# Folding V into Wo for two batches at once, with the contraction filled by stacked Wo parts, from batch 4 on

## What is computed

```
x = x + xattn(x)            q from x, k and v from the normalised 64 context rows
    qk   = einsum('bihd,bjhd->bhij', q, k) * attn_scale
    attn = softmax(qk)
    out  = einsum('bhij,bjhd->bihd', attn, v).reshape(b, -1, 1024) @ Wout
x = x + tanh(layernorm(x) @ W @ aux1 @ aux2 + bias)
```

## Time and profile before

| | |
|---|---|
| median of 3 runs | 2052.41 us (2051.54 to 2052.84) |
| the profiled execution, span | 2049.4 us |
| PE busy | 2024.3 us, 9168 matmuls |
| DVE, ACT, POOL busy | 1523.8, 1320.3, 1342.0 us |
| share of the 16 DMA engines | 74.3% |
| granted TensorE clock | 0.999, at 2.4 GHz |

### The profile page before, as it was taken

The page is one execution under the profiler, slowest core; times in us unless marked ns, Lnnn a source line. Parts: engine busy times, 40 slices in busy tenths (PEclk is TensorE's granted clock), DMA queues, the critical chain, the costliest instruction groups (busy, mean ns, idle before and its releaser), DMA issues.

```text
span 2049.4 us, 31334 instructions
## 1 busy us (share of the span) xinstructions
PE 2024.3 (99%) x9168; PEld 1679.8 (82%) x9168; DVE 1523.8 (74%) x2416; ACT 1320.3 (64%) x3005; POOL 1342.0 (65%) x1463
## 2 busy tenths in 40 slices
PE   8998999999999999999999999999999999999998
PEld 6887878888888888888888888888888888888887
DVE  7567777776777777677777777777777777777776
ACT  4465667666766667666666667666666666666654
POOL 2136767767676776767676776767577676767564
PEclk9999999999999999999999999999999999999999
DMA  7657978889787887878788787878767576666653
GB/s 256 196 184 219 269 226 245 247 231 253 215 229 206 222 222 209 225 202 233 195 229 223 206 224 205 229 201 216 209 186 210 175 206 181 201 184 191 178 169 118
DMA packets 502489, 431.53 MB, mean 211 GB/s; under 512 B 54832, under 2 KB 408240, under 8 KB 502320
## 3 DMA queue, kind: packets, MB, share of 16 engines
q1 hardware_dynamic: 502320, 429.54, 74.3%
HBM read 251.33 MB, written 178.06 MB: 210 GB/s over the span
## 4 chain that ended last, share of the span: by engine, by line
PE 94%; DVE 1%; DMA 1%; ACT 1%; SPq 1%; issue 1%; POOL 0%; DVEq 0%; ACTq 0%
PE bank L161 38%; PE bank L1126 23%; PE bank L166 19%; PE bank L1129 11%; PE bank L830 1%; PE bank L829 1%; DMA stage_more<-ffn_wT_dram 0%; PE bank L827 0%; SPq L306 0%; DMA kv_scratch<-area 0%; ACT bank L388 0%; DMA p_moved<-p_scratch 0%; ACT M_hi L392 0%; PE bank L511 0%; DMA p_scratch<-area 0%
## 5 line engine op out<-in xcount | busy, mean ns | idle before, releaser
L1403 POOL TENSOR_TENSOR area<-area,row_max 128x256 f32<-128x256 f32 x512 | 353.7, 711 | 147.8 <-DVE row_max L1269 147.8
L1126 PE MATMUL bank<-N_hi,pT_hi 128*128 128x512 f32 x1024 | 398.8, 389 | 3.0 <-ACT pT_hi L1172 1.7
L161 PE MATMUL bank<-M_lo,xT_hi 128*128 128x512 f32 x1024 | 398.7, 389 | 0.0
L161 PE MATMUL bank<-M_hi,xT_hi 128*128 128x512 f32 x1024 | 398.6, 389 | 0.0
L1126 PE MATMUL bank<-N_lo,pT_hi 128*128 128x512 f32 x1024 | 398.5, 389 | 0.0
L1172 ACT CAST pT_hi<-turned 128x512 fp32r<-128x512 f32 x256 | 159.1, 621 | 330.4 <-DVE turned L1286 330.4
L1410 POOL TENSOR_TENSOR area<-area,row_inv 128x512 f32<-128x512 f32 x256 | 269.0, 1051 | 114.3 <-DVE row_inv L1278 114.0
L1427 POOL TENSOR_TENSOR area<-area 128x512 f32<-128x512 f32 x127 | 166.0, 1307 | 240.6 <-ACT area L1211 240.5
L1275 DVE TENSOR_REDUCE row_sum<-area 128x8 f32<-128x512 f32 x256 | 174.4, 681 | 167.7 <-ACT area L1167 166.7
L1295 DVE TENSOR_TENSOR pT_lo<-turned,pT_hi 128x512 fp32r<-128x512 f32 x256 | 196.5, 768 | 118.0 <-ACT pT_hi L1172 117.9
L166 PE MATMUL bank<-M_hi,xT_lo 128*128 128x512 f32 x1024 | 273.8, 389 | 0.1
(11 more groups left out here) (178 smaller groups left out, 3916.8 us busy)
## 6 DMA issues: line engine op xcount, KB each, us to landing
p_scratch<-area SPq DMA_DIRECT2D x256, 256.0 KB, 2.6
p_moved<-p_scratch SPq DMA_DIRECT2D x512, 128.0 KB, 4.2
area<-x_dram SPq DMA_DIRECT2D x128, 256.0 KB, 4.5
area<-x_turned_dram SPq DMA_DIRECT2D x128, 256.0 KB, 4.0
x_scratch<-area SPq DMA_DIRECT2D x127, 256.0 KB, 3.0
x_moved<-x_scratch SPq DMA_DIRECT2D x508, 64.0 KB, 3.4
y_dram<-area SPq DMA_DIRECT2D x127, 256.0 KB, 3.4
land<-m_scratch SPq DMA_DIRECT2D x120, 256.0 KB, 2.7
```

The lines of the kernel that those rows point to most:

```text
L161: mm = eng.matmul(ps, sh, mv, start=(n == 0), stop=False)
L1126: pe.matmul(O_ps[:], st(pT_hi, k), n_cols(mv, k), start=(k == 0 and mv is N_hi), stop=False)
L1403: last = pool.tensor_tensor(s, s, row.to_broadcast([P, 2, 4, J2]), ALU.subtract)
```

## The change

Up to batch 3 nothing moves. From batch 4 on N is made for an even batch b0 and its successor together, one pair of heads per slot, in the eight slots 8(b0-1)+2 to 8(b0-1)+9 (called stacked slots: 26 to 33, 42 to 49, and so on to 106 to 113). `wo_scratch` holds, per head, 64 rows of Wo_hi over 64 rows of Wo_lo; it is stored once from slot 10 to 25. Per stacked slot SP issues six small loads of v (`load_v2`, v twice in the partitions, 64 + 64) and two of 128 by 512 (`load_wo2`); ACT and POOL split v (`v2_split_hi`, `v2_split_lo`, 128 by 256); PE makes two matmuls behind each half of O, into two banks (`n2_pe`); ACT and DVE each copy one bank, in two copies of 64 partitions, to `n_stage` (`n2_evacuate`). The space of `n_stage` is that of Wo_hi and Wo_lo. At every border from batch 4 on, ACT and DVE split eight tiles of `n_stage` to `N_hi` and `N_lo` (`n2_hi`, `n2_lo`). Odd batches have the two heads of a pair swapped in N; the DMA that moves P swaps them too. `v_prepare_act`, `diag_lo` and `load_v` are gone for batches from 4 on.

```diff
+        STACKED = 4
+        stacked_at = {TPB * (b0 - 1) + 2 + p: (b0, p) for b0 in range(STACKED, B, 2) for p in range(PAIRS)}
+        def load_v2(sp, b0, p):
+            n = nth_pair(b0, p)
+            sp.wait_ge(s_vp, STACKED + n)
...
+            for half in range(2):
+                dst = v2_raw[half * DH:(half + 1) * DH, :]
+                sp.dma_start(dst[:, 0:P].rearrange("e (b j) -> e b j", b=2), even[:, b0:b0 + 2, :]).then_inc(s_vin, 16)
+                for i in range(2):
+                    sp.dma_start(dst[:, P + i * CTX:P + (i + 1) * CTX], odd[:, b0 + 1 - i, :]).then_inc(s_vin, 16)
+        def v2_split_hi(act, b0, p):
+            n = nth_pair(b0, p)
+            act.wait_ge(s_vin, V_LANDED + 96 * n + 96)
+            act.wait_ge(s_n, n_tiles(n, 0))
+            act.copy(v2_hi[:], v2_raw[:]).then_inc(s_vh, 1)
+        def v2_split_lo(pool, b0, p):
+            pool.wait_ge(s_vh, STACKED + nth_pair(b0, p) + 1)
+            pool.tensor_tensor(v2_lo[:], v2_raw[:], v2_hi[:].bitcast(F32), ALU.subtract).then_inc(s_vp, 1)
+        def n2_pe(pe, b0, p, h):
+            n = nth_pair(b0, p)
+            pe.wait_ge(s_wo2, 32 * n + 32)
+            pe.wait_ge(s_vp, STACKED + n + 1)
+            if n:
+                pe.wait_ge(s_nev, 2 * n)
+            else:
+                pe.wait_ge(s_nl, PAIRS * STACKED)
+            pe.matmul(n2_ps[h][:], v2_hi[:, h * P:(h + 1) * P], wo2[h][:], start=True, stop=False)
+            pe.matmul(n2_ps[h][:], v2_lo[:, h * P:(h + 1) * P], wo2[h][:], start=False, stop=True).then_inc(s_n, 1)
+        def n2_evacuate(eng, copy, b0, p, h):
...
+            copy(stage_of(b0 + h, p)[0:DH], n2_ps[h][0:DH, :])
+            copy(stage_of(b0 + 1 - h, p)[DH:P], n2_ps[h][DH:P, :]).then_inc(s_nev, 1)
+        def n2_hi(act, b):
+            act.wait_ge(s_o, TPB * b)
+            for c in range(PAIRS):
+                act.wait_ge(s_nev, 2 * nth_pair(b - b % 2, c) + 2)
+                act.copy(n_cols(N_hi, c), stage_of(b, c)).then_inc(s_nh, 1)
+        def n2_lo(dve, b):
+            for c in range(PAIRS):
+                dve.wait_ge(s_nh, PAIRS * b + c + 1)
+                dve.tensor_tensor(n_cols(N_lo, c), stage_of(b, c), n_cols(N_hi, c).bitcast(F32), ALU.subtract).then_inc(s_nl, 1)
...
                 tile("BC"[q])
+                if t in stacked_at:
+                    n2_pe(pe, *stacked_at[t], q)
...
-            if m == 1 and 1 < t < T:
+            if m == 1 and 1 < t < TPB * STACKED:
                 fold_n_act(act, t - 1, range(8))
+            elif m == 1 and TPB * STACKED < t < T:
+                n2_hi(act, t // TPB)
...
             sum_tile("C")
+            if t in stacked_at:
+                n2_evacuate(dve, dve.tensor_copy, *stacked_at[t], 1)
```

More of the change, by code:

```diff
@@ L84, in build @@
         N_hi, N_lo = sb("N_hi", PAIRS * D, F32R), sb("N_lo", PAIRS * D, F32R)
+        with nc.sbuf_tensor("n_stage", [P, 2 * PAIRS * D], F32) as n_stage:
+            pass
         Wo_hi, Wo_lo = sb("Wo_hi", PAIRS * D, F32R), sb("Wo_lo", PAIRS * D, F32R)
         W3_hi, W3_lo = sb("W3_hi", DC * D, F32R), sb("W3_lo", DC * D, F32R)
+        with ExitStack() as over:
+            v2_raw = over.enter_context(nc.sbuf_tensor("v2_raw", [P, 2 * P], F32))
+            v2_hi, v2_lo = (over.enter_context(nc.sbuf_tensor(f"v2_{n}", [P, 2 * P], F32R)) for n in ("hi", "lo"))
+            wo2 = [over.enter_context(nc.sbuf_tensor(f"wo2_{i}", [P, D], F32R)) for i in range(2)]
         bdv = sb("bdv", PAIRS * 2 * P, F32R)
@@ new lines, in store_wo @@
+        def store_wo(sp, i):
+            part, h, q = i // 8, i // 4 % 2, 2 * (i % 4)
+            own = slice(h * DH, (h + 1) * DH)
+            sp.dma_start(wo_scratch[q:q + 2, h, part * DH:(part + 1) * DH, :].rearrange("p e d -> e p d"),
+                         (Wo_hi, Wo_lo)[part][own, q * D:(q + 2) * D].bitcast(F32).rearrange("e (p d) -> e p d", p=2)).then_inc(s_wstw, 16)
+        def load_v2(sp, b0, p):
+            n = nth_pair(b0, p)
+            sp.wait_ge(s_vp, STACKED + n)
+            if n == 0:
+                sp.wait_ge(s_n, PAIRS * STACKED)
+            even, odd = kv_scratch[1, p, 0:DH], kv_scratch[1, p, DH:P]
+            for half in range(2):
[3 more added lines that the diff above has]
+                    sp.dma_start(dst[:, P + i * CTX:P + (i + 1) * CTX], odd[:, b0 + 1 - i, :]).then_inc(s_vin, 16)
@@ new lines, in load_wo2 @@
+        def load_wo2(sp, b0, p):
+            n = nth_pair(b0, p)
+            if n == 0:
+                sp.wait_ge(s_wstw, WST_STORES + WO_STORES)
+                sp.wait_ge(s_n, PAIRS * STACKED)
+            for h in range(2):
+                if n:
+                    sp.wait_ge(s_n, n_tiles(n - 1, h) + 1)
+                sp.dma_start(wo2[h][:].bitcast(F32), wo_scratch[p, h]).then_inc(s_wo2, 16)
+        def v2_split_hi(act, b0, p):
[3 more added lines that the diff above has]
+            act.copy(v2_hi[:], v2_raw[:]).then_inc(s_vh, 1)
@@ L879, in load_land @@
             at_least(sp, s_ll, l)
-            if b and j == 1:
+            if 0 < b < STACKED and j == 1:
                 sp.wait_ge(s_vp, b + 1)
@@ L1059, in slot_sp @@
                 load_k(sp, kp + 1)
-            if m == 0 and 0 < t < T:
+            if m == 0 and 0 < t < TPB * STACKED:
                 load_v(sp, t // TPB)
@@ L1083, in slot_sp @@
                 load_land(sp, 6)
-            elif m == 0 and t + 1 < T - TPB:
+            elif m == 0 and t < TPB * STACKED:
                 load_land(sp, t + 1)
+            if t + 1 in stacked_at:
+                load_wo2(sp, *stacked_at[t + 1])
         def slot_pe(pe, t, m):
@@ L1100, in slot_pe @@
                         pe.wait_ge(s_ll, t - 4 + 4 * q)
-                    elif m == 2 and t > 2:
+                    elif m == 2 and 2 < t < TPB * STACKED:
                         pe.wait_ge(s_nl, t + 3 + q)
@@ L1245, in slot_act @@
                 ln1_stats(act, 3, 3)
+            if t in stacked_at:
+                n2_evacuate(act, act.copy, *stacked_at[t], 0)
             evacuate("C")
@@ L1391, in slot_dve @@
                 pT_lo_part(0, t - 1)
[L1392 removed]
+            if m == 0 and 0 < t < TPB * STACKED:
                 diag_lo(dve, bdv, s_vh, s_vp, t // TPB)
[L1394 removed]
+            if m == 1 and 1 < t < TPB * STACKED:
                 fold_n_dve(dve, t - 1, range(8))
+            elif m == 1 and TPB * STACKED < t < T:
+                n2_lo(dve, t // TPB)
         def slot_pool(pool, t, m):
```

39 lines of the change are left out of this document (31 added, 8 removed).

## The result

The change makes the kernel slower: 2093.74 us (median of 4 runs, 2085.95 to 2095.49) against 2052.62 for the kernel before timed beside it (2051.54 to 2054.11). The ratio is 1.0191, interval [1.0172, 1.0209]. The forecast was 2066.0, its range ended at 2090. The profiled execution spans 2091.0 us.

The account below looks back on a forecast made before the run. PE was taken to bound the kernel: -21.8 us of matmuls, +12.8, +6.4 and +16.4 us of stalls after borders give +13.8 on 2052.4, so 2066 us; range 2042 to 2090, the likeliest case 2057 to 2077.

Parts of the forecast that it names:

- The bound, and the reserve behind it: PE sets the time; the other engines are only 0.67 us per slot faster with a small piece, 0.17 without.
- Removed from PE, 21.8 us: 288 border matmuls removed, 192 added in stacked slots: net 96 at 0.2267 us, 21.8 us less PE work.
- They stand between O's addition and the second transposition: DVE's two PSUM copies per stacked slot, 1.25 us, inside the softmax loop, which becomes 14.4 us.
- The borders: Eight DVE subtractions, 5.4 us, lose their matmul cover; PE stalls after borders for 12.8, 6.4 and 16.4 us.
- Rival 1: Border transpositions come 1.5 us earlier, so the gain is kept: 2048, or 2031 with all stalls gone; chance 0.17.
- Rival 3: At borders, DVE subtractions with both inputs in SBUF are slowed by POOL: 28 us more, 2094; chance 0.05.
- Rival 2: In stacked slots, late v or POOL's added row makes the loop 15.4 us, longer than PE: 2086; chance 0.15.
- a DMA is what releases PE: Sign that would prove the forecast wrong: after borders, PE's waits are released by a DMA (or `pT_hi`).
- Added on SP: eight issues. ... I cost it at nothing.: Stacked slots: v's six loads delay P's second write some 1.2 us, but its data is needed after a whole slot.

Follow-up runs that it names:

- all_gone: first_too with the edits of wo_once and thin_border added, so N is wrong; all PE matmuls of the change remain: 2035.89 us, ratio 0.9917.
- thin_border: Changed kernel with the split to N_hi and N_lo at borders from batch 4 on cut to 64 of 512 columns: 2050.63 us, ratio 0.9987.
- two_in_gaps: first_too with two of each border's eight tiles split early, in gaps of ACT and DVE; everything computed: 2073.69 us, ratio 1.0102.
- wo_once: Changed kernel with Wo loaded for the first stacked slot only, later pairs using the same blocks, so N is wrong: 2075.33 us, ratio 1.0105.
- act_early: Changed kernel with Wo loads issued by ACT, v loads behind SP's y store, the first v at the end of slot 25: 2078.50 us, ratio 1.0118.
- first_too: Changed kernel with v loads issued behind SP's y store and the first six last in slot 25; Wo stays on SP: 2083.28 us, ratio 1.015.
- v_in_one: first_too with v laid out twice by 48 DRAM-to-DRAM copies in slots 9 to 24, then one v load per stacked slot: 2090.46 us, ratio 1.0182.
- fold_thin: Kernel before the change, each border tile from batch 4 on made by one matmul of 64 columns, not three of 512: 2070.47 us, ratio 1.0078.

## Why the prediction was wrong

- **The bound, and the reserve behind it**: right. Slots without a stall are exactly 15.01 and 14.10 us long, the loop of the others hides in a stacked slot, and 50 to 58 took 115.6 us (forecast 116.0).
- **Removed from PE, 21.8 us**: right, as `all_gone` shows (20.4 with 1.8 of slot 26 left, the sum within 0.4).
- **"They stand between O's addition and the second transposition"**: the two copies take 1.42 us (at the border of slot 33, 667.96 to the transposition at 669.38), not 1.25, and cost nothing visible in slots with a piece, since 14.5 is still under 15.0.
- **The borders**: the mechanism right, the sum 30.4 in place of 35.6. The term that was off is the 5.4 us of subtractions, read from the earlier trace rows: that row had PE's pace, a tile every 0.68 us, and freed of PE they took 4.8, 0.60 each. With 4.8, 5.8 + 12.7 - 15.9 = 2.6 for an even border (measured 2.8). An odd border came to 0.95, not 1.6, for the same reason. `thin_border` shows that the stalls hang on these subtractions, and `two_in_gaps` that at even borders they go down nearly one for one with them (1.05 of 1.2). Of the 30.4, some 3 us are the lower clock in slots 99 and 123.
- **Rival 1**, the gain kept: false. DVE's subtractions were quicker, as it had it, but by 0.6 us a border and not 1.5. Its limit, 2031 with all stalls gone, is what `all_gone` nearly reached by leaving the work out (2035.9).
- **Rival 3**, DVE slowed by POOL: false, 4.89 us for eight rows and no 0.29 more in any. Where the two met it was POOL that took longer (last section).
- **Rival 2**, a landing that is late: right in kind ("a DMA is what releases PE" was named as what would refute the sum) and wrong in place: it let v lengthen the loop, while in fact Wo held PE itself. That its time, 2086, lies near the measured 2094 is luck.
- **The step that failed: "Added on SP: eight issues. ... I cost it at nothing."** I followed the second write of P, which has a slot to spare, and no further. Behind it in the same queue stand the write of x, a load, a store and the two loads of Wo, which have 8.2 us of the next slot less 4.1 to land. The issues of slots 42 to 49 take SP 8.4 us a slot before (67 us, in slots of 14.1 and one of 19.5) and 13.1 after (105 us). `wo_once` puts the loads' cost at 18.4 us, and `act_early` and `first_too` put slot 26's at 5, though in `first_too` as much was lost again behind it. `v_in_one` shows that it is the time SP spends on v's issues: with five of six gone (78.6 us of issues in slots 42 to 49) PE waits for Wo once, for 0.2 us, though its buffer is still single and the DMA engines as busy (the bytes of v are the same, in rows of 1 KB and no longer of 256 and 512 bytes).
- **A term that had no place in the sum**: the clock. After waits of 4.2, 2.2, 2.0, 2.1 and 1.9 us (slots 26, 43, 59, 99, 123) PE's matmuls ran at 1.2 GHz for some 3 us, which is some 7 us more in the profiled execution, 1.3 to 1.7 at each place. These us are already in the rows of the table. Not each such wait did it: after 2.06 us in slot 115 the clock stayed at 2.4 GHz.

Of the 41.6 us between the two profiled executions, then: -21.8 matmuls, +30.4 borders, +29.1 for slot 26 and late Wo, slow matmuls included, and 4.2 ahead of slot 26 that stay open. Also not settled is how `v_in_one`'s copies lengthen slots 9 to 24. Their issues take 1.94 us a slot (0.64 + 1.30), about what these slots grew by, and stand ahead of the store that frees `evac`, for which PE waits; that this store is the path was not tried.

## What to carry to other kernels

Count a queue's issuing time per slot as you count an engine's: eight more issues of some 0.6 us made SP's queue as long as PE's slot, and the load that stands last paid. Follow each moved issue down to the last one behind it, and ask which has the least time to land. Work that hides under matmuls has no price until the matmuls go; `fold_thin` removed most of 5.4 us of them at each of twelve borders and got nothing back. And a row that keeps step with another engine shows that engine's pace, not its own price.
